# The experts' output bias as a 16-row product into the output banks, in place of an add to the residual on POOL

## The reference

```python
def _L1_ffn_ref(x, Wr, br, W1, b1, g1, be1, m1, v1, W2, b2, g2, be2, m2, v2, Wo, bo):
    feat = jnp.mean(x, axis=0)
    w = jax.nn.softmax(feat @ Wr + br, axis=-1)
    h = jnp.einsum('bfd,edh->bfeh', x, W1) + b1
    h = jax.nn.relu(_bn(h, g1, be1, m1, v1))
    h = jnp.einsum('bfeh,ehk->bfek', h, W2) + b2
    h = jax.nn.relu(_bn(h, g2, be2, m2, v2))
    y = jnp.einsum('bfeh,ehd->bfed', h, Wo) + bo
    return jnp.einsum('bfed,fe->bfd', y, w)
...
t = t + _L1_attn_ref(_ln_t(t), ...)
t = t + _L1_ffn_ref(_ln_t(t), ...)
```

## Time and profile before

| | |
|---|---|
| median of 3 runs | 178.53 us (177.56 to 179.08) |
| profiled execution | 178.39 us |
| its span | 176.6 us |
| mean granted clock | 0.903 |
| PE busy | 149.6 us, 85% of the span |
| PE weight loads | 77.3 us, 44% |
| DVE busy | 115.9 us, 66% |
| ACT busy | 83.1 us, 47% |
| POOL busy | 43.7 us, 25% |
| chain that ended last | PE 60%, DVE 19%, ACT 13%, POOL 4% |
| a quarter of the output, issue to landing | 2.3 us |

### The profile page before, as it was taken

One profiled execution on the slowest core, in us unless ns is written; L12 is line 12 of the kernel. 1 busy time (PEld: TensorE's weight loads), 2 busy tenths in 40 slices (PEclk: granted clock), 3 DMA queues, 4 the chain that ended last, 5 costly groups with the idle time before them and its releaser, 6 DMA issues.

```text
span 176.6 us, 2471 instructions
## 1 busy us (share of the span) xinstructions
PE 149.6 (85%) x830; PEld 77.3 (44%) x830; DVE 115.9 (66%) x396; ACT 83.1 (47%) x141; POOL 43.7 (25%) x45
## 2 busy tenths in 40 slices
PE   7958499999356788669859779999999999999992
PEld 2422233253131374446436546656655564554330
DVE  0595866894676555498986871685551358599992
ACT  0005030310760122546505788988699995397010
POOL 6025202003300206403045590000374000490000
PEclk9996789999876557985896999999999999999999
DMA  5940000000000000000000000000000000010024
GB/s 155 376 165 0 2 4 0 0 4 0 0 2 0 0 4 0 0 0 2 0 4 2 0 0 0 0 4 0 0 0 0 0 4 0 0 58 1 6 59 119
DMA packets 3676, 4.28 MB, mean 24 GB/s; under 512 B 192, under 2 KB 3392, under 8 KB 3536
## 3 DMA queue, kind: packets, MB, share of 16 engines
q1 hardware_dynamic: 3520, 3.92, 6.4%
q10 hardware_dynamic: 144, 0.20, 0.6%
HBM read 3.07 MB, written 1.05 MB: 23 GB/s over the span
## 4 chain that ended last, share of the span: by engine, by line
PE 60%; DVE 19%; ACT 13%; POOL 4%; issue 3%; DVEq 0%; ACTq 0%; POOLq 0%
PE bank L1001 15%; PE bank L1010 8%; PE bank L991 8%; PE bank L873 7%; PE bank L833 5%; ACT y L385 3%; PE bank L890 3%; PE bank L846 3%; PE bank L941 2%; DVE s_ws L599 2%; DVE y L661 2%; ACT xs L432 2%; ACT x L392 2%; ACT y L371 2%; DVE xs L743 2%
## 5 line engine op out<-in xcount | busy, mean ns | idle before, releaser
L1001 PE MATMUL bank<-h,f2s 128*128 128x512 f32 x64 | 33.0, 598 | 1.4 <-DVE xs L743 1.0
L441 ACT ACTIVATE h<-bank,s_bnb,s_bns 128x512 f32<-128x512 f32 x32 | 24.8, 774 | 7.1 <-PE bank L991 7.0
L991 PE MATMUL bank<-xs,f1hi 128*128 128x512 f32 x32 | 20.9, 653 | 1.0 <-DVE xs L743 1.0
L873 PE MATMUL bank<-pad,w 32*64 32x512 f32 x288 | 18.6, 595 | 0.0
L1001 PEld LDWEIGHTS bank<-h,f2s 128*128 128x128 f32 x64 | 11.6, 188 | 6.0 <-ACT h L441 2.6
L840 PE MATMUL bank<-warm 128*128 128x512 bf16 x32 | 13.1, 562 | 1.3 <-ACT y L371 1.3
L991 PE MATMUL bank<-xs,f1lo 128*128 128x512 f32 x32 | 12.6, 394 | 0.0
L833 PE MATMUL bank<-warm 128*128 128x512 bf16 x32 | 10.8, 501 | 1.3 <-POOL warm L334 1.3
L873 PEld LDWEIGHTS bank<-pad,w 32*64 32x64 f32 x288 | 7.3, 130 | 10.0 <-issue 7.5
L890 PEld LDWEIGHTS bank<-par,x 128*128 128x128 f32 x64 | 9.7, 233 | 3.7 <-ACT x L392 2.0
L890 PE MATMUL bank<-par,x 128*128 128x128 f32 x64 | 10.5, 324 | 0.8 <-DVE x L671 0.5
(11 more groups left out here) (274 smaller groups left out, 281.9 us busy)
## 6 DMA issues: line engine op xcount, KB each, us to landing
par<-params SPq DMA_DIRECT2D x1, 1414.0 KB, 10.1
xin<-x SPq DMA_DIRECT2D x4, 256.0 KB, 4.4
out<-act SPq DMA_DIRECT2D x4, 256.0 KB, 2.3
w<-conv_w SPq DMA_DIRECT2D x1, 288.0 KB, 7.0
par<-params ACTq DMA_DIRECT2D x1, 193.5 KB, 3.3
row_par<-row_params SPq DMA_DIRECT2D x1, 80.0 KB, 9.8
```

What stands on the lines that cost most here:

```text
L441: A.activation(h1[n % 3][:], bank[Z1[n % 2]][:], ACT.Relu, bias=tile("bnb", P, 2 * EP)[:, e:e + 1], scale=tile("bns", P, 2 * EP)[:, e:e + ...
L873: ins = T.matmul(bank[CONV1[k][2 * j + h]][at:at + C, :], w1[rows, tap, :], pad[rows, b:b + 2, dy:dy + S, dx:dx + S], start=(tap == 0), st ...
L991: ins = T.matmul(bank[Z1[n % 2]][:], weights[:, e, :], xs[:, k, q, h::2, :], start=(m == 0), stop=(m == 1))
L1001: T.matmul(bank[Z2[n % 2]][:], f2s[:, e, :], h1[n % 3][:], start=True, stop=True).then_inc(z2_done, 1)
```

## The change

`bias.0` leaves the table, and with it the product into the small bank, the copy on DVE, the four adds on POOL and the waits of `finish` for them. Instead the first mix of each output bank is preceded on PE by two 16-row products, one for each half of the bank: the output biases of half q, 16 by 64, times wT, repeated over the four pairs (512 columns). They open the bank (start=True), and no mix does. For bank 4 the first mix now waits for ACT's copy of `wb.1` instead of the copy of the bias.

```diff
@@ layer3, before the product of mix m @@
                 if m % PER_OUT == 0:
 
-                    last, count = {0: (xs_ready, 4 * NK), 7: (tok2_ready, Q * NK), 1: (xs_ready, 4 * NK), 4: (bias_ready, 1)}[OUT[k][q]]
+                    last, count = {0: (xs_ready, 4 * NK), 7: (tok2_ready, Q * NK), 1: (xs_ready, 4 * NK), 4: (small_free, SMALL_AT["wb", Q - 1])}[OUT[k][q]]
                     pe.wait_ge(last, count)
-                T.matmul(bank[OUT[k][q]][h * C:(h + 1) * C, :], wo[:, e, :], held[mixes[m]], start=(e == 0), stop=(e == EP - 1)).then_inc(mlp_done, 1)
+                    pe.wait_ge(rows_loaded, 16)
+                    pe.wait_ge(small_free, SMALL_AT["wt", 0])
+                    turned = tile("wT", Q * E, P).rearrange("p (o n) -> p o n", o=1).broadcast_to([Q * E, PK, P])
+                    for half in range(2):
+                        at = q * P + half * C
+                        T.matmul(bank[OUT[k][q]][half * C:(half + 1) * C, :], r_("bo")[:, at:at + C], turned, start=True, stop=False)
+                T.matmul(bank[OUT[k][q]][h * C:(h + 1) * C, :], wo[:, e, :], held[mixes[m]], start=False, stop=(e == EP - 1)).then_inc(mlp_done, 1)
@@ removed @@
-                for n in range(Q * NK):
-                    q, k = n // NK, n % NK
-                    pairs, pixels = halves(k, q)
-                    G.tensor_tensor(x1[:, pairs, pixels], x1[:, pairs, pixels], bias_ch[:, q:q + 1, :].broadcast_to([P, PK, P]),
-                                    ALU.add).then_inc(t2_biased, 1)
...
-                V.tensor_copy(bias_ch[:], bank[SMALL][:, 0:Q * P].rearrange("p (q n) -> p q n", q=Q)).then_inc(bias_ready, 1)
...
-                dve.wait_ge(t2_biased, n + 1)
...
-                    ins = T.matmul(bank[SMALL][:, q * P:(q + 1) * P], r_("bo")[:, q * P:(q + 1) * P], tile("wT", Q * E, P),
-                                   start=True, stop=True)
@@ two lines of the table @@
-    mix.0 mix.1 mix.2 mix.3 mix.4 mix.5 mix.6 mix.7 bias.0 unit.25 unit.26 unit.27 unit.28 unit.29 unit.30 unit.31 mix.8 mix.9 mix.10
+    unit.27 unit.28 wb.1 unit.29 unit.30 unit.31 mix.0 mix.1 mix.2 mix.3 mix.4 mix.5 mix.6 mix.7 unit.32 mix.8 mix.9 mix.10 mix.11 mix.12
```

More of the change, by code:

```diff
@@ L65 @@
 ORDER = [(s.split(".")[0], int(s.split(".")[1])) for s in """
[L66 to L73, removed]
@@ L78 @@
-    mix.27 mix.28 finish.1 mix.29 mix.30 mix.31 finish.2 finish.3
+    warm.0 warm.1 warm.2 warm.3 warm.4 warm.5 warm.6 silu0.0 warm.7 warm.8 warm.9 warm.10 gn1.0 silu0.1 warm.11 warm.12 gn1f.0 gn1.1
+    warm.13 silu.0 xnorm.0 warm.14 bn.0 silu.1 warm.15 gn1f.1 gn2.0 gn2f.0 xnorm.1 conv.0 norm0.0 conv.1 conv.2 conv.3 gn2.1 conv.4 bnf.0
+    conv.5 conv.6 gn2f.1 norm0.1 s2row.0 conv.7 silu.2 ws.0 conv.8 silu.3 conv.9 conv.10 ws.1 conv.11 conv.12 conv.13 ws.2 ws.3 gn3.0
+    silu.4 conv.14 conv.15 conv.16 gn3f.0 win.0 conv.17 w2.0 gna.0 heat.0 ws.4 gnaf.0 ws.5 ws.6 silu.5 heat.1 heat.2 silu.6 silu.7 ynorm.0
@@ new lines @@
+    wan.0 heat.3 ws.7 heat.4 gate.0 ynorm.1 w3.0 outp.0 gate.1 gn4.0 heat.5 heat.6 gn4f.0 gn3.1 x1.0 gn3f.1 ln1.0 ln1.1 tok.0 heat.7 hn.0
+    heat.8 heat.9 heat.10 win.1 heat.11 hch.0 hn.1 fc.0 coef.0 hch.1 score.0 w2.1 att.0 fc.1 score.1 gna.1 scan.0 ynorm.2 coef.1 heat.12
+    ynorm.3 gnaf.1 att.1 wan.1 scan.1 t2.0 heat.13 gate.2 heat.14 w3.1 t2.1 gate.3 ln2.0 outp.1 gn4.1 gn4f.1 xn2.0 ln2.1 x1.1 xn2.1 xt.0
+    ln1.2 heat.15 tok.1 xt.1 unit.0 ln1.3 hn.2 unit.1 hn.3 unit.2 hch.2 unit.3 fc.2 unit.4 coef.2 score.2 hch.3 unit.5 fc.3 att.2 unit.6
@@ new lines @@
+    coef.3 score.3 unit.7 unit.8 unit.9 att.3 scan.2 unit.10 scan.3 t2.2 unit.11 ln2.2 unit.12 t2.3 unit.13 xn2.2 ln2.3 xt.2 unit.14
+    unit.15 unit.16 unit.17 unit.18 xn2.3 sums.0 unit.19 logits.0 unit.20 unit.21 wt.0 xt.3 unit.22 wb.0 unit.23 unit.24 unit.25 unit.26
+    unit.27 unit.28 wb.1 unit.29 unit.30 unit.31 mix.0 mix.1 mix.2 mix.3 mix.4 mix.5 mix.6 mix.7 unit.32 mix.8 mix.9 mix.10 mix.11 mix.12
+    mix.13 mix.14 mix.15 mix.16 mix.17 mix.18 mix.19 mix.20 mix.21 mix.22 mix.23 mix.24 mix.25 mix.26 mix.27 mix.28 finish.0 mix.29 mix.30
@@ L79 @@
+    mix.31 finish.1 finish.2 finish.3
 """.split()]
@@ L237, in positions @@
             return {s: i + 1 for i, s in enumerate(found)}
-        SMALL_AT = positions({"gn1", "gn2", "s2row", "gn3", "w2", "gna", "w3", "gn4", "score", "sums", "logits", "wt", "wb", "bias"})
+        SMALL_AT = positions({"gn1", "gn2", "s2row", "gn3", "w2", "gna", "w3", "gn4", "score", "sums", "logits", "wt", "wb"})
         STATS_AT = positions({"gn1", "gn2", "gn3", "w2", "gna", "w3", "gn4"})
@@ L1029, in _ @@
                 "sums": lambda k: turn_sums(), "logits": lambda k: logits(), "mix": layer3, "wt": lambda k: weights_transposed(), "wb": weights_spread,
-                "bias": lambda k: bias_product(), "unit": unit,
+                "unit": unit,
             }
```

19 lines of the change are left out of this document (2 added, 17 removed).

## The result

| | before | after |
|---|---|---|
| median of 4 runs | 178.06 us (177.56 to 179.08) | 183.63 us (181.89 to 186.3) |
| ratio, 95% interval | | 1.0273 (1.0166 to 1.038) |
| profiled execution, its span | 178.39, 176.6 us | 181.89, 180.1 us |
| PE busy | 149.6 us | 151.5 us |
| DVE, POOL busy | 115.9, 43.7 us | 111.4, 37.4 us |

The changed kernel is slower: 4.9 us by the ratio (178.06 x 0.0273), 3.5 us in the two profiled executions.

The account below looks back on a forecast made before the run. PE bounds the kernel from 104 us on; before that no engine is full. Span 176.6 + 3.8 (tail: 3.44 - 0.43 + 0.80) + 0.3 (front) = 180.7, with 1.79 around it 182.5 us; range 179.8 to 184.6.

Parts of the forecast that it names:

- the tail: PE after 143.85 us: streaming and changes of shape sum to +3.8 us, bounds +2.6 and +7.25.
- the front: The rearranged first 104 us: +0.45 near 47 us, 0 at 60 to 80, -0.15 at 83 to 100; sum +0.3 us.
- What bounds the kernel: From 104 us on PE is the bound; added PE work lengthens the last 30 us one for one, POOL's savings nothing.
- The stretch: From the end of wb.0 on PE to the end of the last mix; forecast as PE alone, lengthened by +3.8 us.
- Streaming, +3.44 - 0.43: PE's tail: four bias pairs at 0.86 us each add 3.44; the removed bias product saves 0.43.
- Changes of shape, +0.80: PE's tail: 11 changes of tile shape instead of 7, four more at 0.20 us each.
- Cheap change: Rival in PE's tail: bias to mix is no change of shape; tail +2.6, 181.3 us; chance 0.13.
- No pairing: Rival in PE's tail: the two half-bank products run one after the other; tail +7.25, 185.9 us; chance 0.06.
- the walk itself: The chain of the first 104 us followed through the new order with durations of before; early sum +0.3 us.
- The clock falls differently: Rival in the front: L885, L890 and L941 find PE's full clock, 3.65 us less, 178.8 us; chance 0.15.
- The rearrangement is worth more: Rival in the front: for instance ACT's normalisings leave the chain in both places, 1.97 us each; 178.6 us; chance 0.04.

Follow-up runs that it names:

- e2: The kernel before with the changed kernel's order table, bias.0 put behind mix.7 as it was; 189.81 us, ratio 1.0653.
- e4: The changed kernel with biases and wT padded with zeros to 128 rows, giving the bias products the mixes' shape; 183.01 us, one execution.
- e5: The changed kernel with one 16-row product of 128 columns in place of each pair of 64; 184.01 us, one execution.
- e6: The kernel before (bias through DVE and POOL) in the new order table, its bias product right behind wb.0 into idle bank 7; 180.17 us, ratio 1.0086.
- e8: e6 in the order table of before: bias through DVE and POOL, its product right behind wb.0 into bank 7; 178.42 us, ratio 0.9993.
- e7: The changed kernel run once more, nothing changed, on the chip of e6, e8 and e9; 184.02 us, ratio 1.0299.
- e1: The changed kernel with the order table of before, less bias.0; 181.62 us, ratio 1.0204.
- e3: The changed kernel without the eight bias products, so the output lacks the experts' output bias; 179.5 us, ratio 0.999.
- e9: The changed kernel with four more heats (products of zeros) on PE, two behind outp.1 and two behind heat.15; 181.71 us, ratio 1.0214.
- c2: e6 with the same four heats as e9; 178.48 us, ratio 1.0014.

## Why the prediction was right, and where not

The forecast was slower, 182.5 us in 179.8 to 184.6. The profiled execution was 181.89, the median 183.63, and the ratio gives 182.9. That the middle of the forecast is so near is in part luck: the tail was 0.24 us too dear in it, the front about 1 us too cheap.

- **What bounds the kernel**: right. The stretch is PE without gaps in every kernel that I read except e2, and the same stretch stands in the old and in the new order, 32.99 and 32.87. DVE was ahead and POOL's saved 6.7 us were worth nothing.
- **Streaming, +3.44 - 0.43**: right. A pair without a change of shape is 0.86 (e4), and depth gives no discount: 128 rows cost what 16 cost. The Trainium skill says the same in "TensorE: Matmul & The Clock Gate", section "Why this matters for your kernels": a single product of a quarter of the rows takes as long as a full one.
- **Changes of shape, +0.80**: the count of four more was right, the price too high. The stretch grew by 3.56; less 3.01 of streaming, 0.55 is left, 0.14 each. The step that failed is the 0.20. I had read it from L991, L1001 and L978, which are 128 columns wide. Going into a shape of 64 columns costs 0.14 (1.00 - 0.86, and 3.58 - 3.43 is 0.15), which I had read from the mixes too and set aside. By kind: five more changes into 64 columns and one fewer into 128 are 5 x 0.14 - 0.20 = 0.50. The tail's sum was 3.8 and is 3.56.
- **Cheap change** (181.3): fallen, and shown twice, by the loads at 0.81 and by e4, where the same shape brings 0.29 and the 0.9 us back. The sentence of the Trainium skill, "TensorEngine Tiling (Array Packing)", section "Key Properties", that a change of mode drains the engine holds for 16 by 64 against 128 by 64.
- **No pairing** (185.9): fallen by the piece of 1.00 and by e5.
- **The front, +0.3**: near for the profiled execution (wb.0 ends at 143.80 instead of 143.85), too small for the typical one. The ratio leaves 4.9 - 3.56 = 1.3 us for it. e6 against e8 gives 1.7, e7 against e1 1.7 (1.0299 - 1.0204), e3 0.6 (its stretch is 0.8 shorter, its time 0.2 less). The step that failed is that I walked the front with durations of one execution. I let the L941 leave the chain there (-1.94) and put in the waits of DVE, but did not see that `ln2.1` and `tok.1` come onto the chain, with a length that the clock sets: 1.01 to 1.92 and 2.05 to 3.78, nor that PE would stand idle for 2.29 us ahead of `tok.1`, where it had been idle for 0.26. The 2.02 us of idle time ahead of `ln2.1` were there before.
- In the walk itself, w3.0 came at 50.92 (predicted 51.3), and the gates at 86.00, not later than before's 86.03. x1.1 came only 0.26 us later (95.12 against 94.86 of before's chain) and not 1.4, and the winning back behind it was as much smaller; the second layer 2 was at 104.36, within my half microsecond of 104.5. Two errors that cancelled. The early part of the walk was off as well: by the statistics behind outp.0 the new front is 0.20 ahead (56.42 against 56.62), where I had it 0.45 behind. w3.0's product took 0.37 instead of 0.68 and ACT's normalising (1.97) left the chain, while outp.0 had 3.09 on it instead of 2.00. From there the two chains keep step up to the gates.
- **The clock falls differently**: the rival's mechanism exists, its sign was wrong. I looked for a rise at L885 and the first L890. The tokens' L890 stayed at half (3.37 in both), and outp.0 had only its first 0.7 us at the full level (3.09 where e7 has 3.70). The second L941 did find the full level (1.24 us at 85.50), but it had left the chain. What the clock then did to the time was a loss, behind 92 us.
- **The rearrangement is worth more**: fallen as to the time. ACT's normalisings did leave the chain in both places, but the waits behind them stayed, as the prediction held against it: the gates begin at 86.00 where they began at 86.03. Of all kernels in the new order none is below its partner in the old one.

What stays open: by the ratios the front's price is between 0.6 us (e3) and 1.8 (e7, 5.34 less 3.56), and its ratios overlap with their partners' a little. That the clock under `ln2.1` and `tok.1` makes up to 2.84 us of difference is shown in the traces (9.89 against 7.05 us); how much of the price against the old order that is, they do not split, since that order has pieces at half clock there too. That the clock falls there because PE was idle just ahead is supported by e9 and c2 and not shown by more, since the kernel before has the first of the two gaps too. Whether another order with the product in the banks would be free of it was not tried.

## What to carry to other kernels

Where one engine runs without a gap up to the end, work taken from idle engines and given to it costs its full streaming time, however few rows it has; and each change of PE's tile shape adds to that, so pad a small product to its neighbours' shape, or put it beside one of its own shape. An order that puts PE work behind a gap onto the critical path makes the time depend on the clock there, which the durations of one profile don't show: compare the windows of several executions. In a table that all engines follow, look for a copy that waits for a far later product before moving a stage: the engine ahead pays for it with everything queued behind.

## What the runs showed that I had not expected

- The same kernel in its front: 181.88 us at a mean granted clock of 0.905 and 186.34 at 0.867, in e7. The Trainium skill, "TensorE: Matmul & The Clock Gate", section "What's actually happening", warns that the number of slow products varies from run to run, and puts the ramp's penalty under 1% of a typical span. The first fits the times and clocks here. The second is said of the ramp: the four pieces above, 3.26 us of 183, lie in the middle of the program, where the clock falls again while PE is on the chain but not full, and are more than that.
- Going into 64 columns costs 0.14 us and going into 128 costs 0.20 (e5: 1.05 - 0.86), both with the load queue idle for about 0.8 (0.81 and 0.76).
- The order of before has no fixed course of the clock either: from 85 to 92 us it was granted 0.99 in the profiled execution of the kernel before and 0.71 in that of e8, whose table is the same up to there.
